# Attention with relative position bias: keys in tiles of 8 image rows by 16 columns, the row bias by 32-row matmuls

## What is computed

```
rw[x,y,x',y'] = q[x,y] . pos_emb_w[y' - y + 63]      # the column bias: y' is the key's column
rh[x,y,x',y'] = q[x,y] . pos_emb_h[x' - x + 63]      # the row bias: x' is the key's row
probs = softmax over (x',y') of (q.k / sqrt(32) + rw + rh)
out[x,y] = sum over (x',y') of probs * v[x',y']
```

## Time and profile before

| | us |
|---|---|
| median of 3 runs | 8872.92 (8867.76 to 8877.17) |
| the profiled execution | 8869.04 |
| its span, first to last instruction | 8867.2 |
| TensorE busy in the span | 7995.2 (90%) |
| VectorE, ScalarE, GpSimd busy | 6578.0, 4699.9, 6099.3 |
| the rows of the attention, first score to last | 171.6 to 2859.9 |

### The profile page before, as it was taken

One profiled execution on the slowest core, in us unless ns is written; L12 is line 12 of the kernel. 1 busy time (PEld: TensorE's weight loads), 2 busy tenths in 40 slices (PEclk: granted clock), 3 DMA queues, 4 the chain that ended last, 5 costly groups with the idle time before them and its releaser, 6 DMA issues. The chain is left out here.

```text
span 8867.2 us, 126518 instructions
## 1 busy us (share of the span) xinstructions
PE 7995.2 (90%) x42744; PEld 5897.8 (67%) x42744; DVE 6578.0 (74%) x7389; ACT 4699.9 (53%) x12692; POOL 6099.3 (69%) x3153
## 2 busy tenths in 40 slices
PE   6999999999999677999999999968999998888798
PEld 3445445445454336888888888835868778888775
DVE  5666666666565667999999999966867638999634
ACT  3445445445454346777777777713656614454304
POOL 2666666666666247999999999901868807999505
PEclk7999999999999777999999999978999989898888
DMA  5221221221211455444434444452000010000000
GB/s 162 51 51 29 54 49 31 52 51 29 54 29 31 171 194 182 110 105 107 105 106 107 109 104 107 100 233 81 25 24 22 22 45 20 1 1 1 21 9 20
DMA packets 495354, 622.21 MB, mean 70 GB/s; under 512 B 275016, under 2 KB 303056, under 8 KB 486288
## 3 DMA queue, kind: packets, MB, share of 16 engines
q1 hardware_dynamic: 494736, 614.47, 25.2%
HBM read 373.34 MB, written 173.81 MB: 62 GB/s over the span
## 5 line engine op out<-in xcount | busy, mean ns | idle before, releaser
L1652 POOL TENSOR_TENSOR m_c_h<-m_h,m_c 128x2048 f32<-128x2048 f32 x520 | 2340.9, 4577 | 46.5 <-DVE m_h L1639 46.5
L1639 DVE TENSOR_TENSOR_SCAN m_h<-m_decay,m_ps_x 128x1024 f32<-128x1024 f32 x1040 | 2271.3, 2262 | 92.6 <-issue 65.8
L969 DVE TENSOR_REDUCE l_max_by_row<-l_ps_all 128x8 f32<-128x512 f32 x2048 | 1390.0, 689 | 880.8 <-PE l_ps_all L772 875.3
L1552 PE MATMUL m_ps_y<-m_c_h,m_ident 128*128 128x256 f32 x8320 | 1979.8, 381 | 2.1 <-POOL m_c_h L1652 2.1
L901 ACT ACTIVATE l_probs<-l_ps_all 128x512 f32<-128x512 f32 x2048 | 1207.8, 597 | 1243.1 <-PE l_ps_all L804 1162.6
L1552 PEld LDWEIGHTS m_ps_y<-m_c_h,m_ident 128*128 128x128 f32 x8320 | 1509.7, 190 | 175.7 <-POOL m_c_h L1652 4.6
L956 POOL TENSOR_TENSOR l_probs_added<-l_probs 128x512 f32<-128x512 f32 x704 | 917.2, 1303 | 662.8 <-ACT l_probs L901 652.9
L2666 POOL TENSOR_TENSOR s_late<-s_late,s_products 128x1024 f32<-128x1024 f32 x352 | 857.8, 2478 | 318.5 <-ACT s_products L2648 318.5
L956 POOL TENSOR_TENSOR l_probs_added<-l_probs_added,l_probs 128x512 f32<-128x512 f32 x640 | 821.9, 1284 | 346.6 <-ACT l_probs L901 331.7
L2206 POOL TENSOR_TENSOR l_probs_low<-l_probs,l_probs_high 128x512 fp32r<-128x512 f32 x512 | 663.6, 1302 | 561.4 <-ACT l_probs_high L2189 546.7
L1576 ACT ACTIVATE m_b_diagonals<-m_steps,m_b_rows 128x32 fp32r<-128x32 f32 x4160 | 967.0, 306 | 3.1 <-DMA m_b_rows<-b_t 2.9
(11 more groups left out here) (386 smaller groups left out, 12540.2 us busy)
## 6 DMA issues: line engine op xcount, KB each, us to landing
m_delta_u<-du_t SPq DMA_DIRECT2D x1040, 128.0 KB, 3.6
m_c<-c_windows SPq DMA_DIRECT2D x130, 512.0 KB, 4.3
l_q_and_row_bias<-bias_and_low_column_bias SPq DMA_DIRECT2D x64, 512.0 KB, 5.1
du_t<-m_delta_u_high SPq DMA_DIRECT2D x128, 256.0 KB, 3.0
du_t<-m_delta_u_low SPq DMA_DIRECT2D x128, 256.0 KB, 3.0
ys<-m_y SPq DMA_DIRECT2D x256, 126.0 KB, 4.8
m_direction<-ys SPq DMA_DIRECT2D x12, 2048.0 KB, 13.6
l_q_parts<-q_parts SPq DMA_DIRECT2D x32, 512.0 KB, 9.1
```

The costliest lines, as they stand in the source:

```text
L969: dve.tensor_reduce(dst, ps[:, MAX0 + u % 2, :].rearrange("p (x y) -> p x y", y=SIDE), AX.X, ALU.max).then_inc(max_taken, 1)
L1552: ins = pe.matmul(y_ps[:, group % 2, 0:DIRS * SPAN].rearrange("p (d t) -> p d t", d=DIRS), ident[:, :], ch[:, group % CH, :, n, :], start= ...
L1639: dve.tensor_tensor_scan(h[:, u % H, :], decay[:, pair % 2, ct, k % 2, :, :].rearrange("p n t -> p (n t)"), x_ps[:, u % X, :], 0.0, ALU.mu ...
L1652: pool.tensor_tensor(ch[:, group % CH, 2 * pair % DIRS:2 * pair % DIRS + 2, :, :].rearrange("p d n t -> p d (n t)"), h[:, 2 * pair % H:2 * ...
```

## The change

Keys are stored in another order: a tile becomes 8 image rows by 16 columns, eight tiles below one another for each of the four groups of 16 columns. A tile's keys then lie in 16 columns only, so 16 rows of high and 16 of low place the column bias, and they fit beside k.q in one matmul of 128 rows. What is left is the row bias of 8 image rows per tile; it comes from 32 contraction rows, in another matmul of 32 rows. Four tiles form a cycle, and the four 32-row matmuls of a cycle lie on the four row groups of the array, each with its own PSUM bank (`add_rows`, L828). Only after them may ScalarE begin with the four tiles.

- `score` (L820) is now one full matmul a tile; `queries` holds, per row of the work and for each of the four column groups, q high, q low, q high again and the column bias. They are loaded for two rows ahead (`load_queries`, 11 DMAs a row, three slots), so `max_unit` (L792) uses the same tables, and its maxima hold k low and all of the column bias.
- `add_rows` needs the shifted row bias in 128 rows: `copy_rows` (8 DMAs a row, as before, to `rx`).
- The maxima lie by cell of 16 columns: `reduce_unit` (L1002) writes 32 values per 512, and `take_maxima` gets a further reduce over 4 (L1006).
- The high half of the shifted row bias is made by ScalarE (`make_high`, L945), not by VectorE.
- Jobs: two a row (cycles 1 and 3), not 16 in two rows. `load_tables` is cut into four parts, in the second to fifth row of a head.
- 14 buffers for `probs`, 4 for the sums, 4 score banks; `fold_up` goes to the bank `TURNED`.
- In the projection, `normalise` works by 512 tokens, in an order by column group, k is stored as 512-byte pieces, and v once an image.

```diff
-                ql = m.sb("q_and_row_bias", [P, 2, GROUPS, TW], F32R)
+        keys, queries = m.sb("keys", [P, 2, L], F32R), m.sb("queries", [P, 3, GROUPS, TW], F32R)
...
-            def score(row, i):
...
-                if n >= 3:
-                    pe.wait_ge(expd, n - 2)
-                o, keys, queries = ps[:, n % 3, :], slice(i * P, (i + 1) * P), slice(j * TW, (j + 1) * TW)
-                pe.matmul(o, km[:, it % 2, keys], qm[:, it % 2, queries], start=True, stop=False)
-                pe.matmul(o, k2[:, it % 2, keys], ql[:, slot, i // (KT // GROUPS), :], start=False, stop=True).then_inc(scored, 1)
+            def score(row, c, k):
...
+                if row * KT + i >= GROUPS:
+                    pe.wait_ge(expd, row * KT + i - GROUPS + 1)
+                pe.matmul(ps[:, k, :], keys[:, it % 2, i * P:(i + 1) * P], queries[:, row % 3, c // 2, :], start=True, stop=False)
+
+            def add_rows(row, c):
+
+                if c == 0:
+                    rows_loaded(pe, row)
+                for k in range(GROUPS):
+                    part = slice(k * D, (k + 1) * D)
+                    ins = pe.matmul(ps[:, k, :], cells[part, c % 2, :], rx[part, row % 2, :], start=False, stop=True)
+                ins.then_inc(scored, 1)
...
             def take_maxima(row):
                 dve.wait_ge(max_taken, (row + 1) * UNITS)
+                chain.link(dve.tensor_reduce(mx64[:, :, :], mx4[:, :, :, :].rearrange("p q g x -> p q x g"), AX.X, ALU.max))
                 dve.wait_ge(bias_turned, row + 1)
...
+            def make_high(row):
+
+                act.wait_ge(shifted, row + 1)
+                if row:
+                    rows_loaded(act, row - 1)
+                act.activation(rh[:, :], r1[:, :], ACT.Copy).then_inc(high_made, 1)
...
             for row in range(ROWS):
                 it, j = row // NTB, row % NTB
-                if row + 1 < ROWS:
-                    copy_common(row + 1)
+                if row + 2 < ROWS:
+                    load_queries(row + 2)
+                if j == NTB - 1 and it + 2 < ITS:
+                    load_qc(it + 2)
                 if row >= 1:
                     send_sums(row - 1)
                     spread_inverses(row - 1)
-                    store(row - 1)
-                if j == 1 and it + 1 < ITS:
-                    load_tables(it + 1)
+                if 1 <= j < 5 and it + 1 < ITS:
+                    load_tables(it + 1, j - 1)
                 if row + 1 < ROWS:
                     copy_rows(row + 1)
+                if row >= 1:
+                    store(row - 1)
```

More of the change, by code:

```diff
@@ L657, in copy_rows, with load_qc @@
-            def copy_rows(row):
-                for first, part, made in ((D, rh, high_made), (D + NEAR, rl, shifted)):
+                if part < 3:
+                    sp.dma_start(f(keys[part * D:(part + 1) * D, k, :]), k_parts[part // 2, rows, tokens]).then_inc(tables_in, 16)
+                else:
+                    sp.dma_start(vv[:, k, :, :], v_heads[it].rearrange("p (k d) -> p k d", d=D)).then_inc(tables_in, 16)
+            def load_qc(it):
+                b, h = it // HEADS, it % HEADS
+                tokens, rows = slice(b * L, (b + 1) * L), slice(h * D, (h + 1) * D)
+                if it:
+                    sp.wait_ge(filled, it * JOBS)
+                for n in range(4):
+                    sp.dma_start(f(qc[n * D:(n + 1) * D, :]), q_parts[n // 2, rows, tokens]).then_inc(qc_in, 16)
@@ L659, in copy_rows @@
+            def copy_rows(row):
+                if row >= 2:
+                    sp.wait_ge(scored, batches_at(row - 2, BATCHES - 1))
+                for first, part, made in ((0, rh, high_made), (NEAR, rl, low_made)):
                     sp.wait_ge(made, row + 1)
                     for g in range(GROUPS):
-                        sp.dma_start(f(ql[first:first + NEAR, row % 2, g, :]), f(part[g * NEAR:(g + 1) * NEAR, :])).then_inc(ql_in[row % 2], 16)
+                        sp.dma_start(f(rx[g * D + first:g * D + first + NEAR, row % 2, :]), f(part[g * NEAR:(g + 1) * NEAR, :])).then_inc(row_in[row % 2], 16)
@@ new lines, in job, with job_taken @@
+                    if n < NTB:
+                        table, moving = ew, by_column[:, at, :]
+                    else:
+                        table, moving = eh, qc[:, at * SIDE:(at + 1) * SIDE]
+                    ins = pe.matmul(ps[0:SIDE, bank, k * SIDE:(k + 1) * SIDE], table[:, SIDE - 1 - at:2 * SIDE - 1 - at], moving, start=True, stop=True)
+                ins.then_inc(filled, 1)
+            def job_taken(it, n):
+                pe.wait_ge(copied, it * JOBS + n + 1)
+                pe.wait_ge(split, splits_to(it, n + 1))
@@ L880, in _ @@
+            for c in range(BATCHES, BATCHES + 2):
+                for n in weighed_in(c):
+                    weigh(ROWS - 1, n)
             fold_up(ROWS - 1)
```

493 lines of the change are left out of this document (242 added, 251 removed).

## The result

Median 8601.61 us in 4 runs (8591.76 to 8615.49), beside 8875.02 of the kernel before (8867.76 to 8877.17, 4 runs): a ratio of 0.9694, 95% interval 0.9678 to 0.9711. Forecast were 8604. The profiled execution took 8596.49 us, against 8869.04.

What follows compares the result with a forecast made beforehand. TensorE alone was taken to bound an undisturbed row (38.9 us). Seven heads at -34.0 (-238), the last head -19, the projection +4 and the attention's start -12 gave -265: 8604 us, full range 8480 to 8850.

Steps and rivals of the forecast that it cites:

- Full matmuls, block, weighings in pairs: TensorE per head: 256 full matmuls gone -58.9, 64 blocks of four 32-row matmuls +28.8, weighings sharing shape changes -7.2 us.
- the serial rival: The four 32-row matmuls run one after the other, a block taking 1.1 us: 8812 us in all, chance 0.08.
- The rival that each of four pays its own change: Each 32-row matmul of a block pays its own change of shape, block 1.7 us: about 9110 us, chance 0.12.
- The stall: Small copies queued behind ten table loads on SyncE's queue; tables in parts and earlier queries save 19.9 us a head.
- ScalarE's turn: TensorE waits for ScalarE's exponentials of four tiles, a loop of 3.7 us against 3.5: +12 a head.
- VectorE: The third maximum unit of cycle 5 waits for VectorE's reduces, 0.8 us a row: +6.4 a head.
- The row bias on its way: Row bias copies from cycle 5 to the next row come late behind table parts, 0.6 us a row: +4.8 a head.
- The other two rivals: Hand-off waits of 6 us a row, 8790, chance 0.10; SyncE's queue with copies 3 us late, 8757, chance 0.08.
- my 23 a head: The forecast waits of TensorE per head: ScalarE's turn 12, VectorE 6.4 and the row bias 4.8 us.
- A block of 0.35 with a third of the waits: Fast end of the forecast's own range: -58 us a head, about 8430, unlikely all at once, so 8480.
- Last head: The attention's last head, without stall or jobs: -19 us.
- Ahead of the first score: Before the attention's first score: projection +4 us for small DMA pieces, attention start -12 us with smaller tables.

Runs made afterwards that it cites:

- one_group: The changed kernel with all four 32-row matmuls of a cycle on the first row group of the array: 8835.91 us, 0.9956.
- before_tables_split: The kernel before, with the next head's table loads in four parts behind the row's small copies, second to fifth row of a head: 8727.53 us, 0.9831.
- max_adjacent: The changed kernel with the maxima laid so that the further reduce reads its four values next to one another: 8550.25 us, 0.9636.
- short_units: The changed kernel with each maximum unit's reduce reading 8 of every 16 keys, the others left out of the maximum: 8482.23 us, 0.9562.
- tables_after: The changed kernel with the table parts issued behind the row's copies and the store, not ahead of them: 8578.79 us, 0.9679.
- high_on_vector: The changed kernel with the high half of the shifted row bias made by VectorE, not ScalarE: 8585.94 us, 0.9687.

## Why the prediction was right, and where its terms were not

The sum came out at -265 by the forecast and at -272.7 in the span of the profiled execution, 7.8 of that behind the attention. Point by point, per head of the first seven:

- *Full matmuls, block, weighings in pairs* (-58.9, +28.8, -7.2). Right. The block measures 0.44, not 0.45 (+28.2). Two weighings on end take 1.86 up to the next full matmul, where two single ones take 2 x 1.00 (1446.41 to 1447.41 in the earlier trace rows), and one change in and one slow step behind them go, 0.09 and 0.10: a pair saves 0.33, -8 a head, where I took 0.3. The serial rival (1.1) is what `one_group` shows, 1.12, and the change doesn't do it. The rival that each of four pays its own change falls with it. There are 24 changes of shape a row in place of 22; the block adds 0.44 where one step is 0.23, so 0.21 for changes: 0.10 going into it and 0.20 going on to the weighing, less the 0.09 that stood there before. The 0.05 of load in that rival's sum is shown by no run; the four in a row of `one_group` leave nothing for it. The Trainium skill (TensorEngine Tiling (Array Packing), "Key Properties") says that a change of tiling mode drains TensorE; the trace agrees that it costs something, and shows it once a block and not once a matmul.
- *The stall* (-19.9): -19.7 by `before_tables_split`. Right, and shown by itself.
- *ScalarE's turn* (+12): wrong in size. TensorE is idle for ScalarE for 2.8 us in all, but 204 weight loads of the scores waited for it, and the steps at them are longer, by some 5.5 a head in all (my count in the trace of the change). They stand where I had put them, behind the copies of the jobs (58) and behind `make_high` (128), and hardly one is in a plain cycle, where I had 0.2 each. The step that failed is "Three exponentials take 1.99, so four 2.65": their spacing there was TensorE's. Four take 2.06, the loop is then 3.1 and not 3.7, and TensorE's own 3.5 is longer. Taking an instruction of 0.6 out of ScalarE's cycle 6 brought 16 us, not the 40 to 50 of a bound there.
- *VectorE* (+6.4): 56.8 / 8 = 7.1 of visible wait, where it was 10.8 / 8 = 1.4: +5.7. The size was right by two errors that cancel: the reduce over 1024 took 2.04, not 1.2, and at 1.2 there would have been almost no wait, as `max_adjacent` shows.
- *What I had not seen at all*: the third and fourth maximum unit of most cycles come while both banks are with VectorE, whose reduces of 0.69 are as long as before, while the cycle is shorter. Their weights come late, and the next step is 0.10 longer. Counted in the traces, apart from units right behind a change of shape, the change has 103 such units a head and the kernel before 28; with the steps ahead of them they lengthen a head by 14 and by nearly 7, so the change adds about 7. `short_units`, with the steps at 0.22 and 0.23, shows that VectorE is the cause.
- *The row bias on its way* (+4.8): 53.8 / 8 = +6.7. I had put the lateness down to table parts; `tables_after` gives those about a third, and the inverses' place in the queue has more.
- With these the sum is -58.9 + 28.2 - 8 - 19.7 + 5.5 + 5.7 + 7 + 6.7 = -33.5 a head; measured are -237.0 / 7 = -33.9. No term is known to better than about 1 us, so that the two meet so closely is in part chance.
- *The other two rivals.* TensorE stands idle for 122 us in the seven heads, 2.2 a row, and waits for GpSimd's sums 2.6 us in all, so the hand-off of 6 a row didn't come; the copies are 0.85 a row late and not 3.
- *Sums of the forecast that don't add up.* A block of 0.35 with a third of the waits gives -56 a head and not -58, and the serial rival's -57 takes the last head for one like the others; by its own terms it is -53. Neither moves the forecast.
- *Last head* -19 forecast, -19.1 measured. *Ahead of the first score*: SyncE's first issue in the attention stands at 87.81 in place of 86.57, 1.2 later (forecast +4), and from there to the first score it took 10 less (forecast -12).

So the time was right because the terms of TensorE and the stall were, which carry it. That the waits came to about my 23 a head (now 25) owes something to luck: ScalarE's 12 were 5.5, and a term of 7 was missing.

## What to carry to other kernels

Before a matmul is rebuilt, look for the lump in a DMA queue: over half of this gain was to be had by cutting ten loads into four parts behind the small copies, and moving the lump only moved the stall to the next small transfer. When a kernel's bound is shortened, read the weight loads' waits too, not only TensorE's idle time: here a held weight load lengthened the next step by 0.10 us, and that was counted as busy. A spacing read from a timeline is an engine's own speed only if nothing paced it. A wait found after a change is its cost only less the same wait before.

## What the hardware showed that I had not expected

- Four fp32r matmuls of 32 rows by 512 columns on four row groups and four banks last 0.51 together, as long as one full matmul alone (0.50), with 0.43 to the next shape; on one row group it is 1.12 to the next shape.
- The step behind a matmul whose weights were held is 0.34 where it is otherwise 0.23, whether VectorE's bank or a change of shape held them.
- A float32 reduce over 1024 elements of SBUF takes 2.04 us when the reduced values lie 64 elements apart and 1.22 when they are adjacent, on the same engine and for the same count. For the PSUM reduces the form of the output made no difference (689 ns with 8 results, 685 with 32).
- Exponentials of 0.60 start 0.49 apart when four tiles are ready at once.
- The same subtraction `shift_low` has a mean of 1590 ns before, 1209 after, and 674 in `high_on_vector`. The cause stays open; none of these kernels was made to ask for it:

```profile
L1021 DVE TENSOR_TENSOR l_row_bias_low<-l_row_bias_shifted,l_row_bias_high 64x512 fp32r<-64x512 f32 x64 | 43.1, 674 | 0.1
```
